# P V with V stationary and P transposed moving, even and odd heads in two halves of PSUM

## The reference, cut to what matters

```python
sim = jnp.einsum('bhwid,bhwjd->bhwij', bq, bk)      # 8 heads of 64, window 128, own and previous window
sim = jnp.where(mask, -jnp.finfo(sim.dtype).max, sim)
attn = jax.nn.softmax(sim, axis=-1)
out = jnp.einsum('bhwij,bhwjd->bhwid', attn, bv)    # P V
...
x = x + o @ wo
h = shift_token(x)                                   # then layer norm, gate, value, down
```

## Time and profile before

| | us |
|---|---|
| median of three runs | 2399.89 |
| span of the profiled execution | 2415.6 |
| TensorE (PE) busy | 2209.6 |
| VectorE (DVE) busy | 1073.0 |
| ScalarE (ACT) busy | 894.3 |
| GpSimd (POOL) busy | 683.0 |
| P V matmuls (L1300) busy, 1792 of them | 231.4 |

### The profile page before, as it was taken

One profiled execution on the slowest core, in us unless ns is written; L12 is line 12 of the kernel. 1 busy time (PEld: TensorE's weight loads), 2 busy tenths in 40 slices (PEclk: granted clock), 3 DMA queues, 4 the chain that ended last, 5 costly groups with the idle time before them and its releaser, 6 DMA issues.

```text
span 2415.6 us, 28757 instructions
## 1 busy us (share of the span) xinstructions
PE 2209.6 (91%) x8902; PEld 1292.4 (54%) x8963; DVE 1073.0 (44%) x2012; ACT 894.3 (37%) x2175; POOL 683.0 (28%) x664
## 2 busy tenths in 40 slices
PE   4773999994999999999999999999999999999997
PEld 3532666662555555555555555555555555555553
DVE  5543222222454454454444535444454444453541
ACT  0011333331444534343534444344535343434432
POOL 5063000003532252432224315222252422231310
PEclk9965999996899999999999999999999999999998
DMA  8332212212100010100001001000010200000000
GB/s 258 105 114 89 61 59 61 61 53 46 27 9 1 1 27 1 42 12 28 1 1 16 12 27 27 18 11 1 1 27 1 44 9 18 1 0 1 1 15 12
DMA packets 71768, 78.19 MB, mean 32 GB/s; under 512 B 17156, under 2 KB 63704, under 8 KB 71640
## 3 DMA queue, kind: packets, MB, share of 16 engines
q1 hardware_dynamic: 56104, 58.68, 7.7%
q0 software_dynamic: 12672, 17.87, 3.6%
q10 hardware_dynamic: 2864, 0.01, 0.1%
HBM read 48.19 MB, written 28.35 MB: 32 GB/s over the span
## 4 chain that ended last, share of the span: by engine, by line
PE 61%; DVE 5%; issue 5%; ACT 3%; POOL 2%; DMA 1%; ACTq 0%; DVEq 0%; POOLq 0%
PE pj L1340 12%; PE pj L1252 11%; PE sc L1277 8%; PE ob L1300 7%; PE pj L1346 7%; PE pj L1314 4%; PE pt L1287 3%; DVE swapped L1524 3%; PE pj L1260 2%; PE pj L1327 1%; PE sc L1272 1%; PE pj L1242 1%; PE pj L1321 1%; POOL x1tok L1471 1%; PE pj L1308 1%
## 5 line engine op out<-in xcount | busy, mean ns | idle before, releaser
L1482 POOL TENSOR_TENSOR qksq<-qkraw 128x512 f32<-128x512 f32 x128 | 160.3, 1271 | 874.9 <-ACT qkraw L1381 874.9
L1405 ACT ACTIVATE prob<-sc,nm 128x256 f32<-128x256 f32 (+1 forms) x512 | 224.2, 443 | 449.5 <-DVE nm L1538 449.2
L1252 PE MATMUL pj<-wqkv,xT 128*128 128x512 f32 x768 | 350.4, 606 | 10.2 <-issue 10.2
L1340 PE MATMUL pj<-h,w 128*128 128x512 f32 (+1 forms) x704 | 337.9, 605 | 6.4 <-DVE h L1564 4.5
L1277 PE MATMUL sc<-kT,qT 64*128 64x256 f32 (+1 forms) x1024 | 266.2, 381 | 14.7 <-ACT kT L1395 5.4
L1524 DVE TENSOR_TENSOR swapped<-qkraw,tabs 128x256 f32<-128x256 f32 x256 | 256.0, 1038 | 0.0
L1300 PEld LDWEIGHTS ob<-vv,pT 128*128 128x128 f32 x1792 | 221.1, 193 | 59.9 <-issue 41.6
L1252 PEld LDWEIGHTS pj<-wqkv,xT 128*128 128x128 f32 x768 | 143.7, 193 | 191.0 <-issue 190.6
L1300 PE MATMUL ob<-vv,pT 128*128 128x64 f32 x1792 | 231.4, 275 | 9.9 <-ACT pT L1173 7.4
L1277 PEld LDWEIGHTS sc<-kT,qT 64*128 64x128 f32 x1024 | 164.3, 189 | 102.1 <-issue 88.9
L1538 DVE TENSOR_REDUCE nm<-sc 128x2 f32<-128x512 f32 (+1 forms) x256 | 158.5, 620 | 129.4 <-PE sc L1277 128.5
(11 more groups left out here) (246 smaller groups left out, 2642.6 us busy)
## 6 DMA issues: line engine op xcount, KB each, us to landing
xt<-slots_x SPq DMA_DIRECT2D x72, 128.5 KB, 2.1
slots_y<-yt SPq DMA_DIRECT2D x72, 128.0 KB, 1.7
xin<-in_x_dram SPq DMA_DIRECT2D x8, 512.0 KB
w1m<-in_L_ffn_w_dram SPq DMA_DIRECT2D x8, 512.0 KB
w2m<-in_L_ffn_w_dram SPq DMA_DIRECT2D x8, 512.0 KB
x1tok<-in_x_dram SPq DMA_DIRECT2D x8, 512.0 KB, 4.5
x_after_moe<-x1tok SPq DMA_DIRECT2D x8, 512.0 KB, 2.6
x1out<-x_after_moe SPq DMA_DIRECT2D x8, 512.0 KB, 4.4
```

Of the source, the lines that this page charges most:

```text
L1252: mm = pe.matmul(o[:, :], xs(s, c, w * P, P), wqkv[:, l, c, k * INNER:(k + 1) * INNER], start=(c == 0), stop=(c == DC - 1))
L1340: mm = pe.matmul(o[0:P if j == NJ - 1 else HJ[j], :], cols, h[:, c, :], start=(c == 0), stop=(c == DC - 1))
L1405: ins = a.activation(prob[:, g % 4, hh, 0:n], sc[g % 2][:, hh, 0:n], ACT.Exp, bias=nm[:, g % 4, hh:hh + 1], accum_out=rs[:, st["win"] % 2, ...
L1482: pool.tensor_tensor(qksq[:, k * INNER:(k + 1) * INNER], src, src, ALU.mult).then_inc(squared, 1)
```

## The change

The P V product is turned round: V of one head (128 keys x 64 channels) becomes the stationary operand and P transposed (128 keys x 128 queries) the moving one. The result comes out transposed, channels on partitions: even heads in partitions 0 to 63 of `ob`, odd heads in 64 to 127. One pv step now covers two groups, so pv:0 and pv:1 take the place of four steps, with twice the weight in the merge, and within a step each even head's matmul is followed by the odd head's. The step waits for the `pT` copies of both its groups. turn_o and `on` are gone. A new step turn_r, before pv:1, has VectorE invert the sums and spread them over 64 columns each (`rr_wide`), TensorE transpose that, and ScalarE copy it to `rb`; VectorE then writes `oT` as `ob` times `rb` after pv:1. wo waits for that product. `h` is laid over `xsq`.

```diff
-    score:3 pv:0 turn_o pv:1 turn_p:2 turn_p:3 turn pv:2 pv:3
+    score:3 pv:0 turn_p:2 turn_p:3 turn turn_r pv:1
...
-            elif kind == "turn_o":
-                if w:
-                    out.append(dict(kind=kind, s=s, l=l, w=w - 1))
+            elif kind == "turn_r":
+                out.append(dict(kind=kind, s=s, l=l, w=w))
...
-    out = [st("turn_o", w=NW - 1)] + room + [st("wo", c=c) for c in range(DC)] + room + [st("mean")] + room
+    out = room + [st("wo", c=c) for c in range(DC)] + room + [st("mean")] + room
...
-    weight = {"qkv": 1.2}.get(step["kind"], 1.0)
+    weight = {"qkv": 1.2, "pv": 2.0}.get(step["kind"], 1.0)
...
-USES = dict(qkv=3, turn=2, turn_o=1, wo=1, mean=1, var=1, gate=1, value=1, down=1, load=DC, rotate=DC, out=NW)
+USES = dict(qkv=3, turn=2, turn_r=1, wo=1, mean=1, var=1, gate=1, value=1, down=1, load=DC, rotate=DC, out=NW)
...
-        if kind in ("qkv", "rope", "norm", "turn", "turn_o"):
+        if kind in ("qkv", "rope", "norm", "turn", "turn_r"):
...
-            st["grp"] = c.take("grp_" + kind, 1)
+            st["grp"] = c.take("grp_" + kind, 2 if kind == "pv" else 1)
...
+        if kind == "wo":
+            st["win"] = c.n["grp_pv"] // 4
...
-        for what in ("qkv", "turn", "turn_o", "wo", "gate", "value", "load"):
+        for what in ("qkv", "turn", "turn_r", "wo", "gate", "value", "load"):
...
-    for what in ("turn", "turn_o"):
-        assert c.n["last_" + what] - start["last_" + what] == per["use"]
+    assert c.n["last_turn"] - start["last_turn"] == per["use"]
...
-            on = sb("on", [P, INNER])
+            rr_wide = sb("rr_wide", [P, H, DH])
+            rb = sb("rb", [P, IC, P])
...
-            h = sb("h", [P, DC, T])
+            h = xsq
...
-            ob = ps("ob", [P, INNER])
+            ob = ps("ob", [P, IC, P])
...
-                            pe.wait_ge(pt_taken[g % 2], at(g // 2, i, GRP // 2, 1, 1))
+                            for par in range(2):
+                                pe.wait_ge(pt_taken[par], at(g // 2, i, GRP // 2, 1, 1))
...
+                            slots = [(w % 2, win % 4)] + ([(1 - w % 2, (win - 1) % 4)] if w else [])
...
-                                head = head_of(st["g"], hh)
-                                slots = [(w % 2, win % 4)] + ([(1 - w % 2, (win - 1) % 4)] if w else [])
...
-                                    mm = pe.matmul(ob[:, head * DH:(head + 1) * DH], pT[:, g % 4, hh, slot, :],
-                                                   vv[:, v_at, head * DH:(head + 1) * DH],
-                                                   start=(k == 0), stop=(k == len(slots) - 1))
-                            mm.then_inc(pv_done, 1)
-                        elif kind == "turn_o":
-                            pe.wait_ge(o_ready, at(st["win"], i, WIN, 1, 1))
+                                    for par in range(2):
+                                        head = head_of(2 * st["g"] + par, hh)
+                                        mm = pe.matmul(ob[par * DH:(par + 1) * DH, head // 2, :],
+                                                       vv[:, v_at, head * DH:(head + 1) * DH],
+                                                       pT[:, (g + par) % 4, hh, slot, :],
+                                                       start=(k == 0), stop=(k == len(slots) - 1))
+                            mm.then_inc(pv_done, 2)
+                        elif kind == "turn_r":
+                            pe.wait_ge(inverted, at(st["win"], i, WIN, 2, 2))
...
-                                mm = pe.transpose(o[:, c * P:(c + 1) * P], on[:, c * P:(c + 1) * P], ident[:, :])
+                                mm = pe.transpose(o[:, c * P:(c + 1) * P],
+                                                  rr_wide[:, 2 * c:2 * c + 2, :].rearrange("p h d -> p (h d)"),
+                                                  ident[:, :])
...
-                            wait_taken(pe, st["turn_o_use"], i)
+                            pe.wait_ge(o_ready, at(st["win"], i, WIN))
...
-                        elif kind == "turn_o":
+                        elif kind == "turn_r":
...
+                            wait(a, o_ready, at(st["win"], i, WIN))
...
-                            a.copy(oT[:, :, w * P:(w + 1) * P], o[:, :].rearrange("p (c t) -> p c t", c=IC)
+                            a.copy(rb[:, :, :], o[:, :].rearrange("p (c t) -> p c t", c=IC)
...
-                        elif kind == "pv" and st["g"] == 3:
+                        elif kind == "turn_r":
...
+                            v.wait_ge(exp_done, at(win, i, WIN, 4, 4))
+                            v.reciprocal(rr[:, :], rs[:, win % 2, :]).then_inc(inverted, 1)
+                            v.wait_ge(inverted, at(win, i, WIN, 2, 1))
+                            v.tensor_copy(rr_wide[:, :, :], rr[:, :].unsqueeze(2).to_broadcast([P, H, DH])
+                                          ).then_inc(inverted, 1)
+                        elif kind == "pv" and st["g"] == 1:
+                            win = st["win"]
+                            wait_taken(v, st["turn_r_use"], i)
...
-                            v.reciprocal(rr[:, :], rs[:, win % 2, :]).then_inc(inverted, 1)
-                            v.wait_ge(inverted, at(win, i, WIN, 1, 1))
-                            v.tensor_tensor(on[:, :].rearrange("p (h d) -> p h d", h=H),
-                                            ob[:, :].rearrange("p (h d) -> p h d", h=H),
-                                            rr[:, :].unsqueeze(2).to_broadcast([P, H, DH]), ALU.mult
+                            v.tensor_tensor(oT[:, :, w * P:(w + 1) * P], ob[:, :, :], rb[:, :, :], ALU.mult
```

## The result

The changed kernel takes 2441.49 us (median of four runs, 2439.68 to 2448.27), the kernel before 2400.23 us in runs beside it. The ratio is 1.0177, interval [1.0162, 1.0191]: about 41 us slower, where +21 was forecast. The profiled execution of before began its attention part 12 us later for a reason that lies in the expert part, so I compare from the first qkv matmul to the end: 1837.5 us before, 1875.0 after, +37.4.

A forecast was written before the change was run, and what follows sets the result against it. TensorE (PE) was taken as the bound, busy 91% of the span. Its own account -10 (152 + 35 - 197), bare windows +22 and other moves +9 gave +21 on 2399.9: 2421 us, range 2374 to 2468.

The forecast's parts named there:

- How two halves run: P V matmuls on two column halves: partial overlap taken, 152 us of stream against 197 before; bounds 113 and 195.
- The forecast's own mark: P V starts in the changed profile: the prediction is wrong if a pair of heads takes under 0.27 us.
- the middle case: P V halves partly overlap, the second part holding the odd head's load; 0.32 us a pair, 2421 us, chance 0.40.
- rival 1: P V halves fully side by side, 0.22 us a pair; -18 us in all, 2382 us, chance 0.32.
- Changing the shape: TensorE entering and leaving the narrow matmul shape at 128 pv steps: 35 us added.
- rr_wide's own length: VectorE's spreading copy in turn_r, 64 times: 0.36 to 0.69 us each, 0.55 taken.
- The walk: Bare window followed step by step: TensorE waits 2.0 us before pv:0 and 0.4 before turn_r; window ends 1.0 later.
- The bare windows: 17 windows with nothing between score:2 and turn: pv:0 waits for both copies; +22 us correction.
- What else moves, +9: Remaining waits: var +7, windows with one step covering group 1's copy +4, wo at the end -2.
- var after mean: var comes sooner after mean, leaving less cover for `xc` and `xsq`: +7 us on waits of 9.5.
- Rival 2: P V halves do not overlap at all: +64 us, 2464 us, chance 0.28.
- Rival 3: Waits larger or smaller than walked: moves each case by 10 us or so, no case of its own.

The follow-up runs named there:

- e1: The changed kernel with each pv step doing all even heads' matmuls before all odd ones; ratio 1.0374 to the kernel before.
- e6: The changed kernel with two extra TensorE matmuls, result overwritten, before pv:0 of each sequence's last window; ratio 1.0129 to the kernel before.
- e2: The old product (P stationary, turn_o) in the changed kernel's order, weights and double pv steps; ratio 1.0464 to the kernel before.

## Why the prediction was wrong

Taken in the prediction's own steps:

- **How two halves run: wrong, the favourable way.** "Its rule is what the loads in the trace do" failed. The earlier trace rows showed loads held behind a matmul over the full width, and that says nothing of a load for the other half. The forecast's own mark for this came in: a pair under 0.27, at 0.22. P V busy time is 133, where it was to be near 150 to 200 and never below 110. Stream, changes of shape and rests went down by 72 us together, -102 + 14 + 17, where the middle case had -10 and rival 1 had -49; its full overlap still let the odd half run one matmul behind the even one, and the starts are 7 ns apart. The Trainium skill ("TensorE: Matmul & The Clock Gate", section "The mechanism") has loads pulled ahead of matmuls in flight for other row groups or the background weights; the runs agree that it happens, 1.02 us a step. The same section limits such overlap to different row groups and has matmuls start and end in program order. Both column halves here use all 128 rows and overlap, and in e1 a later matmul starts first, so there the measurement decides.
- **Changing the shape: about right.** 35 was forecast; the account has 14 for the shape and 17 in small rests, which hold the exposed first loads and tails, 31 in all.
- **rr_wide's own length: right.** 459 ns, inside the bounds of 0.36 to 0.69. **When it runs: wrong, and the wrong way round.** The walk gave 0.4 us in each of 17 bare windows, some 7, and let a feed-forward step in between cover the wait. Measured, the bare windows have none of it (0.09 us in one), and the 19.2 us, 16 waits of up to 2.4, are where feed-forward steps stand. I priced what VectorE does after it hears of turn_r, and not what is queued ahead of it there: the product for `hid`, standing on the very matmul that was to be the cover, and `hnorm`, standing on `rstd`.
- **The bare windows: right in the main.** The wait of 2.0 is 2.05. For full overlap the walk ended 0.37 later than the earlier trace rows. The window of the earlier trace rows itself, and one more, before and then after (same columns as above):

```profile
1439.34:1462.03 22.69, 21.56 (x100) 13.20 (x100) 10.62 (x15) 10.57 (x30) 9.41 (x9) 1.00 0.18 55
1449.28:1472.01 22.73, 19.96 (x101) 11.39 (x101) 11.19 (x17) 10.58 (x30) 9.63 (x9) 1.00 0.20 63
...
1327.93:1346.23 18.30, 17.90 (x92) 11.77 (x93) 11.40 (x17) 8.88 (x26) 8.55 (x7) 1.00 0.17 43
1337.88:1356.28 18.40, 16.29 (x92) 9.96 (x93) 11.74 (x18) 8.88 (x26) 9.28 (x8) 1.00 0.21 48
```

They grew by 0.04 and 0.10. At the same clock such a window was hardly a loss, but no gain either: the 1.6 us less of TensorE's work became a longer wait.

- **What else moves, +9: the term that was too small.** var after mean: 9.5 to 15.3, +6, where +7 stood. But the covered windows were never walked with the new weights. The waits that came there: 13.7 on the bank behind `gelu` and its table load, which no line of the prediction has, nearly all of the 19.2 on `rr_wide`, and 6 more on GpSimd's `roped` (9.5 to 15.8). The waits for `pT`, with those on "issue", rose from 9.9 to 44.4. Of these, 36.8 lie in the bare windows, 29 more than before, where the walk had 17 x 1.6 = 27 more. One of 4.27 is in the last pass, where `gelu` and its table load stand ahead of the copy, and three are of 1.0. All idle stretches together went up by 89 us in the account, where the steps held +31 (22 + 9). This sum of waits, 22 + 9 against 89, is the step that failed against the forecast, by 58 us.
- **The clock: missing.** The text noted "at full clock" for the earlier trace rows and took it for granted afterwards. The account has +20 us. e6 speaks for the waits before pv:0 as one cause: the time falls when they are filled. For the other waits it isn't shown.
- **The sum.** Forecast -45 (stream) + 35 + 31 = +21. Measured -102 + 31 + 89 + 20 = +38 for an attention part that grew by 37.4. The gain was 62 us larger than the steps had it, the waits 58 us and the clock 20 us. With the waits right and the overlap still wrong the forecast would have been some 40 us too high (-10 + 89 against +38); with the overlap right and the waits still wrong it would have had the wrong sign. The sign came out by two errors that nearly cancel.
- **The rivals.** Rival 1 had the mechanism and missed the time by 59 us (2382), since its waits were the same +31 and it had no clock. Rival 2 (2464) is excluded by the step of 1.02. Rival 3 was said to move each case by 10 or so; this was where the case was decided, at +58.

That forecast and time lie only some 20 us apart is luck: two errors of about 60 us nearly cancel, and what is left is about the size of the clock's term.

Not settled: why e2 has so much more time at 1.2 GHz than the kernel after, with idle stretches that are smaller in sum (109.8 against 135.8 us, over 0.4 us each), and what decides whether a wait is followed by the lower level. Not tried: an order that leaves feed-forward steps for the bare windows, which e6 suggests would be worth more than its idle time.

## What to carry to other kernels

Two half-width matmuls whose outputs go to different column halves should alternate in the program; here, with eight matmuls for each half, this was worth 1 to 2% against grouping them, and with four nothing. When a schedule is rewoven by weights, walk every kind of window with the queues of all engines, not the bare ones alone: a short operation comes as late as what stands ahead of it in its engine's order, and a step put in to cover a wait can bring work of its own that lengthens it. On an engine that bounds the kernel, price a wait with the clock that follows it, and test it by filling the wait with idle work.

## What the runs showed of the hardware that was not expected

- Matmuls on two column halves run side by side with float32 operands: sixteen instructions of 128 columns in 1.02 us when alternated, 1.51 us when grouped, where one after the other is 16 x 0.109 = 1.74. In the grouped order the other half starts ahead of three matmuls that come before it in the program.
- Waits of some 2 us between steps often go with the granted level of 1.2 GHz in what follows, about half of them in the kernel after. Eight transposes took 1.67 us instead of 0.87 behind a wait of 2.04, and the attention part of the kernel after spent 108 us at that level, against 54 before.
- More work on the bounding engine made the kernel faster: 27 us of matmuls whose result is overwritten, put into waits, gave 0.0048 back (11.5 us; 1.0177 to 1.0129).
- Spreading 8 values per partition over 512 took VectorE 0.46 us within SBUF, nearer the bound of half a plain copy (0.36) than I took it.
